# Feed-forward output combine: from GpSimd to VectorE, and half of it deferred into the next slab

## What is computed

```python
xn = _layernorm(x, axis=-1)
s = _L0_attn_ref(xn, w_qkv, w_out, b_out)
#   q,k,v = split(xn @ w_qkv.T); softmax(causal(q @ k.T * 512**-0.5)) @ v @ w_out.T + b_out
g = _silu(_L0_ffn_ref(xn, w_gate, w_up, w_down))
#   (silu(xn @ wg.T) * (xn @ wu.T)) @ wd.T, w* = int * (1/127)
x = x + s * g
```

## Time and profile before

| | us |
|---|---|
| median of the two runs | 1991.55 |
| the two runs | 1847.15, 2135.95 |
| profiled execution, its own time | 1838.77 |
| its span, slowest core (core 3) | 1837.2 |
| spans of the eight cores | 1826.1 to 1837.2 |
| mean granted TensorE clock, all cores | 0.951 to 0.956 |

### The profile page before, as it was taken

One profiled execution on the slowest core, in us unless ns is written; L12 is line 12 of the kernel. 1 busy time (PEld: TensorE's weight loads), 2 busy tenths in 40 slices (PEclk: granted clock), 3 DMA queues, 4 the chain that ended last, 5 costly groups with the idle time before them and its releaser, 6 DMA issues.

```text
span 1837.2 us, 20552 instructions; the slowest of 8 cores (1826.1 to 1837.2 us)
## 1 busy us (share of the span) xinstructions
PE 1617.2 (88%) x7748; PEld 778.1 (42%) x7748; DVE 403.5 (22%) x708; ACT 258.6 (14%) x415; POOL 82.1 (4%) x48
## 2 busy tenths in 40 slices
PE   4788799978888888899999699999699999799994
PEld 3555544434444443344444244444244444344442
DVE  5333222132222222122200322200222200222100
ACT  2323211122222222011000110001001001000001
POOL 0000000000000000000001200002200003000004
PEclk9888899979999998899999899999899999899997
DMA  4112010025556530333522433423433423333323
GB/s 140 35 35 69 1 35 12 1 69 92 92 92 103 93 69 24 77 73 81 133 74 67 129 81 77 129 75 96 106 73 77 133 80 116 85 80 70 109 80 120
DMA packets 236113, 146.17 MB, mean 80 GB/s; under 512 B 202929, under 2 KB 211377, under 8 KB 235442
## 3 DMA queue, kind: packets, MB, share of 16 engines
q1 hardware_dynamic: 234674, 123.89, 24.9%
q0 software_dynamic: 768, 18.88, 7.1%
q10 hardware_dynamic: 576, 2.10, 0.4%
HBM read 146.94 MB, written 35.65 MB: 99 GB/s over the span
## 4 chain that ended last, share of the span: by engine, by line
PE 82%; DVE 4%; ACT 4%; DMA 3%; POOLq 3%; issue 3%; ACTq 0%; DVEq 0%; SPq 0%
PE psA L247 54%; PE psA L941 9%; PE psB L676 5%; PE psB L941 4%; PE psC L941 4%; PE psB L742 4%; POOLq L973 2%; POOLq L1007 2%; DMA xin<-x 1%; DVE xnT_lo L448 1%; DMA wub<-wub_scr 1%; DMA wof_st<-woutT 1%; ACT oaT_hi L700 1%; ACT oaf L682 1%; ACT xnT_hi L441 1%
## 5 line engine op out<-in xcount | busy, mean ns | idle before, releaser
L247 PE MATMUL psA<-xnT_hi,wgb 128*128 128x512 f16 x768 | 296.4, 386 | 52.8 <-DMA wub<-wub_scr 50.5
L247 PE MATMUL psA<-xnT_lo,wgb 128*128 128x512 f16 x768 | 296.0, 385 | 0.0
L247 PE MATMUL psA<-xnT_hi,wub 128*128 128x512 f16 x768 | 291.1, 379 | 0.0
L247 PE MATMUL psA<-xnT_lo,wub 128*128 128x512 f16 x768 | 291.1, 379 | 0.0
L857 DVE SCALAR_TENSOR_TENSOR hfs<-psA,hsc 128x512 f32<-128x512 f32 x96 | 66.4, 692 | 785.6 <-PE psA L247 492.0
L849 ACT ACTIVATE hsc<-psA,zeroc 128x512 f32<-128x512 f32 x96 | 66.1, 689 | 600.6 <-PE psA L247 587.0
L247 PEld LDWEIGHTS psA<-xnT_hi,wgb 128*128 128x128 f16 x768 | 76.3, 99 | 149.5 <-issue 62.5
L941 PE MATMUL psA<-wdb,hT_hi 128*128 128x512 f16 x384 | 115.3, 382 | 10.9 <-DVEq L1007 10.9
L941 PE MATMUL psA<-wdb,hT_lo 128*128 128x512 f16 x384 | 116.4, 385 | 0.0
L247 PEld LDWEIGHTS psA<-xnT_lo,wgb 128*128 128x128 f16 x768 | 76.1, 99 | 92.8 <-issue 5.5
L247 PE MATMUL psA<-xnT_hi,wqh 128*128 128x512 f16 x256 | 100.8, 394 | 15.4 <-DVEq L1007 15.4
(11 more groups left out here) (109 smaller groups left out, 1649.0 us busy)
## 6 DMA issues: line engine op xcount, KB each, us to landing
wgb<-wgb_scr SPq DMA_DIRECT2D x96, 256.0 KB, 3.4
wub<-wub_scr SPq DMA_DIRECT2D x96, 256.0 KB, 3.9
wdb<-wdb_scr SPq DMA_DIRECT2D x96, 256.0 KB, 2.6
xt<-x SPq DMA_DIRECT2D x16, 512.0 KB, 3.7
sscr<-stl SPq DMA_DIRECT2D x16, 512.0 KB, 3.2
sin<-sscr SPq DMA_DIRECT2D x16, 512.0 KB, 5.3
xin<-x SPq DMA_DIRECT2D x16, 512.0 KB, 6.7
out<-otl SPq DMA_DIRECT2D x16, 512.0 KB, 3.0
```

The source lines that it names most:

```text
L247: k.op("te", lambda e, lf=lf, rf=rf, j=j, n=n, pf=psum_ap_fn: e.matmul(pf(), lf(), rf(), start=(j == 0), stop=(j == n - 1)), inc=(inc if j ...
```

## The change

GpSimd's semaphore `gq` goes; multiply and add of the combine are issued on VectorE, and the waits that named gq name VectorE's `ve`. The body of the combine becomes a function `emit_comb`. For tt 0 and 1 it is called at the end of the slab, followed by `emit_sx_load(tt + 2)`. For tt 2 and 3 it is put into a list, and the list is worked off at the beginning of hidden tile h=2 of the next slab, ahead of that tile's instructions and behind those of h=1, in all engines' lists. After the last slab it is worked off at once.

```diff
+    pending_combs = []
+
     for s4 in range(NSLAB):
         ...
         for h in range(NH):
+            if h == 2 and pending_combs:
+                for f in pending_combs:
+                    f()
+                pending_combs.clear()
             dF_h = dF_mark[h]
         ...
             if ve_comb.get(tt % 2) is not None:
-                k.wait("sy", "gq", ve_comb[tt % 2])
+                k.wait("sy", "ve", ve_comb[tt % 2])
         ...
-        for tt in range(4):
-            g = s4 * 4 + tt
-            gb = gtl if tt % 2 == 0 else gtl2
-            k.wait("se", "pe", pe_down_tt[tt])
+
+        def emit_comb(tt, g, gb, pdt, dlt, s4=s4):
+            nonlocal out_n, ve_comb_last
+            k.wait("se", "pe", pdt)
             if s4 == 0 and tt == 1 and out_n == 1:
                 k.wait("se", "dS", 16 * NT)
             if ve_comb.get(tt % 2) is not None:
-                k.wait("se", "gq", ve_comb[tt % 2])
+                k.wait("se", "ve", ve_comb[tt % 2])
         ...
-            k.wait("gp", "se", se_gtl[tt])
-            k.wait("gp", dl_tt[tt][0], dl_tt[tt][1])
+            k.wait("ve", "se", se_gtl[tt])
+            k.wait("ve", dlt[0], dlt[1])
             if out_n >= 2:
-                k.wait("gp", f"dO{out_n % 2}", 16 * (out_n // 2))
-            k.op("gp", lambda e, tt=tt, gb=gb: e.tensor_tensor(
+                k.wait("ve", f"dO{out_n % 2}", 16 * (out_n // 2))
+            k.op("ve", lambda e, tt=tt, gb=gb: e.tensor_tensor(
                 otl.ap()[:, tt % 2, :], sin.ap()[:, tt % 2, :], gb.ap(), ALU.mult))
-            k.op("gp", lambda e: e.drain())
-            k.op("gp", lambda e, tt=tt: e.tensor_tensor(
+            k.op("ve", lambda e: e.drain())
+            k.op("ve", lambda e, tt=tt: e.tensor_tensor(
                 otl.ap()[:, tt % 2, :], otl.ap()[:, tt % 2, :], xin.ap()[:, tt % 2, :],
                 ALU.add))
-            k.drain_inc("gp", "gq")
-            ve_comb[tt % 2] = k.cnt["gq"]
-            ve_comb_last = k.cnt["gq"]
-            k.wait("sy", "gq", ve_comb[tt % 2])
+            k.drain_inc("ve", "ve")
+            ve_comb[tt % 2] = k.cnt["ve"]
+            ve_comb_last = k.cnt["ve"]
+            k.wait("sy", "ve", ve_comb[tt % 2])
             k.dma("sy", lambda g=g, tt=tt: out_d.ap()[g * 128:(g + 1) * 128, :],
                   lambda tt=tt: otl.ap()[:, tt % 2, :], f"dO{out_n % 2}")
             out_n += 1
-            if tt + 2 < 4:
+
+        for tt in range(4):
+            g = s4 * 4 + tt
+            gb = gtl if tt % 2 == 0 else gtl2
+            if tt < 2:
+                emit_comb(tt, g, gb, pe_down_tt[tt], dl_tt[tt])
                 emit_sx_load(tt + 2)
+            else:
+                pending_combs.append(
+                    lambda tt=tt, g=g, gb=gb, pdt=pe_down_tt[tt],
+                    dlt=tuple(dl_tt[tt]), em=emit_comb: em(tt, g, gb, pdt, dlt))
+    for f in pending_combs:
+        f()
+    pending_combs.clear()
```

More of the change, by code:

```diff
@@ L218, in build_program @@
     for s in ("dC", "dG", "dX0", "dX1", "dWq0", "dWq1", "dWv", "dWo", "vw", "dS", "dL0", "dL1", "dO0", "dO1",
-              "dF0", "dF1", "dD0", "dD1", "pe", "ve", "se", "gq"):
+              "dF0", "dF1", "dD0", "dD1", "pe", "ve", "se"):
         k.sem(s)
```

## The result

The changed kernel takes 1794.67 us in the median of 11 runs (lowest 1788.43), the kernel before 1844.33 us in 10 (lowest 1836.42). The ratio is 0.9752 with a 95% interval of 0.972 to 0.9784: 2.5% faster. The profiled executions, which the sum was made for, took 1838.8 and 1788.4 us: 50.4 us less, where 50.6 had been summed. The higher times of both kernels belong to executions in which cores of one or both dies ran at a lower granted clock, and they are left out of every ratio here.

A forecast was written before the change was run, and what follows sets the result against it. TensorE was taken to bound the kernel, stalled by weight loads queued behind stores awaiting GpSimd. 42.5 + 5.1 - 3.0 + 6.0 = 50.6 us off 1838.8 gave 1788.2, stated as 1790 with 2 us for offset; range 1777 to 1817.

The forecast's parts named there:

- The stalls, 42.5 us: TensorE's three waits for weight tile wub, 13.8 us into a slab: 14.72, 15.53 and 12.25 us, to be removed.
- The low clock, 5.1 us: TensorE resumes at 1.2 GHz behind each of the three stalls; the lost 2.4+1.9+0.8 us were to be regained.
- VectorE's price: A 128x1024 combine operation takes 1.23 us on VectorE against 2.34 on GpSimd; a combine 2.6 us against 4.9.
- The backlog in front of the pair: 3.14 MB of stores and s/x loads precede the h=2 weight load, which lands at 1017.2 to 1018.7, wanted 1018.2.
- 1.0 us per boundary: Stall left at each of three slab boundaries, h=2 and h=4 together; 3.0 us charged in all.
- the sign of being right: At 13.8 us into a slab, no TensorE wait over 3 us.
- h=4: Its weight load, behind the deferred combines and out 3, lands at 1032.1 against 1032.0 wanted: 0.1 us late.
- rival C: VectorE combines as slowly as GpSimd; h=4's pair 4.6 us late plus clock, no tail gain: 1812 us, chance 0.05.
- The tail: Last slab's combines on VectorE, xin flight taken as 6.5 us: span ends 6.0 us earlier (4 to 8).
- B: At h=2 the weight pair lands behind the bulk: 4.7 us stall plus low clock per boundary, 1806 us, chance 0.13.
- D: The h=2 pair is slow in itself, queue position not the cause; only the tail is won: 1833 us, chance 0.03.
- E: Slower, 1876 us: deferred combines hold VectorE ahead of h=2's product, whose bank h=4 needs; chance 0.03.

The follow-up runs named there:

- e3: Kernel before, with only the stores of tiles 2 and 3 and their waits moved behind the h=2 and h=3 weight loads in the sync queue; profiled execution 1825.7 us.
- e4: Changed kernel, with the s/x loads of tiles 2 and 3 moved behind the h=2 weight pair in the sync queue; ratio to the kernel before 0.973.
- e6: Changed kernel with four buffers instead of two for s, x, silu and output, s/x loads issued in the down projection; ratio to the kernel before 0.967.
- e5: Changed kernel with the multiply of combines 2 and 3 done three times, about 5.2 us per combine instead of 2.6; profiled execution 1814.5 us.
- e2: Changed kernel with the combine's multiply and add back on GpSimd, combines 2 and 3 still deferred; ratio to the kernel before 0.983.
- e7: Changed kernel with four buffers instead of two for s, x, silu and output, but no combine deferred; ratio to the kernel before 0.973.
- e10: The changed kernel unaltered, run again beside the kernel before on the same chip; ratio to the kernel before 0.9788.

## Why the prediction was right

**The cause.** The h=2 pair stood behind the fourth store, and position, not transfer, cost the time. e3 shows it alone: nothing but the place of two stores per boundary is changed.

**The total: luck in part.** Measured 50.4, summed 50.6. Core by core the two profiled executions differ by 46.8 us (core 1) to 55.3 (core 3); core 3 was the slowest before and core 1 is now, and it is by this that the two slowest differ by 50.3. On core 3, for which the sum was made, the parts are 40.1 us of stalls (forecast 42.5 - 3.0 = 39.5), 7.7 of matmul time (5.1), 5.2 of tail (6.0), and 2.3 by which its feed-forward began earlier, in a part of the program that both kernels share (none forecast). The mechanism and the largest term held; the other three were off by 0.8 to 2.6 us each, partly against one another.

**The stalls, 42.5 us.** On core 3, the one of the earlier trace rows, the waits for wub at the boundaries went from 42.5 to 2.4 us; on core 1, now the slowest, from 39.6 to 4.7.

**The low clock, 5.1 us.** From the first gate matmul to the last down matmul core 3 took 1065.8 us before (747.6 to 1813.3) and 1017.9 after (745.3 to 1763.2): 47.8 less, of which 40.1 are waits for wub. Its other waits there are the same in both, 10.9 and 10.8 us for VectorE, 2.1 for ScalarE. The other 7.7 are time of the same 4608 matmuls, so this term was sized too low. Core 3 before, then after:

```profile
747.50:1813.40 1065.90, 1010.15 (x4608) 453.09 (x4608) 186.81 (x288) 84.91 (x125) 57.77 (x25) 0.97 0.35 90
...
745.20:1763.40 1018.20, 1002.49 (x4608) 451.06 (x4608) 204.29 (x313) 84.87 (x125) 0.00 (x0) 0.99 0.36 95
```

About 6.0 of the 7.7 lie right behind the three stalls: in the 10 us behind each, 40, 35 and 38 matmuls started before, and 47 behind the short waits after, 28 slots of 0.216 us. Behind the first stall the windows of the earlier trace rows end at 1034.7, while slots of twice the length went on to 1036.1. Where the other 1.6 us lie wasn't found.

**VectorE's price.** 1225 and 1226 ns measured, 1.23 forecast. The combine took 2.6 us: 1000.69 to 1003.22 plus the signal.

**The backlog in front of the pair** is the term that was sized too low. The pair landed 14.9 us after the slab's start, where 12.8 to 14.3 had been worked out, and some tenths more for its signal. DMA rates of the changed kernel, 1002 to 1022 us in slices of 0.5 us:

```profile
GB/s 0 0 0 0 319 410 344 49 139 377 213 115 90 156 213 369 360 401 418 410 426 426 410 396 344 286 266 219 143 43 1 132 247 262 247 179 13 0 0 0
```

From 1004 the 3.14 MB of bulk are through at about 1014.3, which is 11.9 us into the slab, the upper end of the forecast; the trough (49 to 213 GB/s, one slice of 377 in it) lasts 4 us, from 1005.5 to 1009.5, and ends 6.2 us after the first store's issue at 1003.32. The forecast had put its end 2.8 us behind that issue, though in the earlier trace rows it ended about 5 us behind it; no row gave the shorter time. What ends the trough stays open. Then the pair runs at a falling 344 to 143 GB/s for 2.5 us, and 3.0 us pass from the end of the bulk to its landing, where 1.9 to 2.4 had been taken. By the rule of the Trainium skill ("DMA: Bandwidth & Descriptors", section "Queues, rings and completion order"), ring order and completion behind earlier writes, the pair has to end behind the bulk; the trace agrees: 7.36 us from issue to landing against 3.7 us for a lone pair, and the sharing that would have had it in by 1017 of the forecast's scale did not come. e4 and e6 show that the bulk is the reason: without the four s/x loads in front the wait at h=2 is zero on all cores.

**1.0 us per boundary** was 1.3, 2.5 and 0.9 on core 1: 4.7 against 3.0, and the range over the cores is 2.2 to 5.8. The largest single one, 3.2 us on core 7, is just over the 3 us named as the sign of being right. The second on core 1 also brought the low clock, where 1.00 had been expected. Windows of the changed kernel, core 1, behind the wait of 2.50 us:

```profile
1273.00:1277.00 4.00, 3.96 (x11) 1.54 (x12) 3.60 (x3) 0.00 (x0) 0.00 (x0) 0.57 0.47 132
1277.00:1280.00 3.00, 3.00 (x16) 1.37 (x14) 1.23 (x2) 0.69 (x1) 0.00 (x0) 1.00 0.49 197
```

11 matmuls in 4 us where 18 fit: 1.6 us for a wait of 2.5.

**h=4.** 0.1 us had been charged; there was none. Combine 3 ended at 1024.2 and the h=4 pair went out at 1024.88, just behind the end of h=2's matmuls. The margin is as thin as worked out: e5, 5.2 us later, waits 3.8 us where rival C had 4.6.

**The tail.** 18 us after the last matmul were forecast, 19.0 measured (1767.9 to 1786.9; before 23.9), so the gain is 4.9 and not 6.0 us. The step that was off is xin's flight with the blocks closer together: 6.5 assumed, 7.19 measured. The chain of the changed kernel there:

```profile
1773.32 7.19 DMA xin<-x
...
1780.68 1.23 DVE otl L977
...
1781.98 1.23 DVE otl L980
```

**The rivals.** B had the right mechanism at a third of its price; about its full price, 4.7 us, stands in e2 and e3 (3.4 to 7.2 us per boundary), where the bulk is released by GpSimd. C is e5. D is excluded by e3, and by the 7.4 us in which the pair came even behind the bulk. E's threshold was not reached anywhere, and its wait, TensorE at h=4 for a bank that VectorE still holds, shows in no run, not even with the combine doubled.

## What to carry to other kernels

Where one queue issues both the loads that the bound engine needs next and stores that wait for a slow helper, ask for each load what stands ahead of it in program order: here moving two stores per boundary removed 25 of 41 us, with no engine any faster. Then count the bytes ahead of it: behind 3 MB of bulk a pair that lands in 3.7 us took 7.4, and more buffers let the bulk go at another time. Spread it there one load at a time, since in blocks it only makes the next stream late.

## What had not been expected of the hardware

How long TensorE stood idle didn't by itself say whether it went on at the low clock. Of the waits for wub at h=2 to h=4 in the kernels up to e7 and in e10, all from 0.9 to 1.9 us kept the granted clock at 1.00 over the 4 us behind them, and all of 3.9 us and more were followed by 0.50 to 0.66. Between the two it went either way: 0.57 behind 2.24 us (e5, core 1) and 1.00 behind 2.20 us (e5, core 5); 0.50 behind 3.83 us (e5, core 0) and 1.00 behind 3.57 us (e5, core 3). What decides it, no run here shows. Nor does the low clock always start with the first matmul: behind 3.02 us (e4, core 3) that one still took 0.38 us and the next 0.59; behind 3.83 us (e5, core 0) the first took 0.59. In the changed kernel (cores 0, 1 and 3, first slab) the wait of 2.8 us at the down projection's start had the low clock too, 0.67 over the 4 us behind. First the window of e4, core 3:

```profile
1026.00:1030.00 4.00, 3.85 (x11) 1.44 (x12) 2.70 (x4) 0.00 (x0) 0.00 (x0) 0.57 0.54 146
```

and that of e5, core 0:

```profile
1033.40:1036.40 3.00, 2.96 (x8) 1.03 (x9) 0.00 (x0) 0.00 (x0) 0.00 (x0) 0.50 0.51 87
```

And e5, core 3, behind 3.57 us: first matmul and window.

```profile
1039.01 0.38 PE L247 MATMUL psA<-xnT_hi,wgb 128*128 128x512 f16 x1 [3.57 <-DMA wub<-wub_scr]
...
1039.00:1043.00 4.00, 3.99 (x19) 1.87 (x20) 0.00 (x0) 0.22 (x1) 0.00 (x0) 1.00 0.47 106
```

So a wait of 2 to 4 us cost nothing more in some places, and in others, as on core 1 behind its 2.5 us, more than half as much again, after TensorE had resumed.
